# Last norm moved into the attention stage and into the expert blocks of a transformer layer with a mixture of experts

## What is computed

```python
mod = (_silu(c) @ wmod).reshape(16, 6, 1, -1)
sa, ca, ga, sb, cb, gb = (mod[:, 0], ..., mod[:, 5])
h = _layernorm(x) * (1 + ca) + sa
x = x + ga * attention(h, Wq, Wkv_down, Wk_up, Wv_up, Wo)
h = _layernorm(x) * (1 + cb) + sb
# router: top two of 8 experts, softmax over the two, 1280 rows an expert
y = einsum(gelu(einsum(h[tok], W1) + b1), W2) + b2
out = zeros_like(h).at[tok].add(y * gate) + h
x = x + gb * (layer_norm(out) * gamma + beta)
```

## Time and profile before

| | us |
|---|---|
| median of 3 runs | 1331.41 |
| lowest, highest | 1328.3, 1337.59 |
| span of the profiled execution | 1329.8 |
| its attention stage, to the last router sum | about 1031 |
| its routing | 1031 to 1115 |
| its expert blocks | 1115 to 1260 |
| last scatter and last norm | 1260 to 1329.8 |

### The profile page before, as it was taken

How to read it: one execution, slowest core, us unless ns; L and a number is a source line. 1 busy time by engine, 2 the same in 40 slices (tenths; PEclk the granted TensorE clock), 3 DMA queues, 4 the chain that set the end, 5 groups by cost and what they waited for, 6 DMA issues and landing times. The chain is left out here.

```text
span 1329.8 us, 23668 instructions
## 1 busy us (share of the span) xinstructions
PE 1153.5 (87%) x5959; PEld 770.8 (58%) x5960; DVE 975.3 (73%) x2248; ACT 748.2 (56%) x1454; POOL 936.3 (70%) x1075
## 2 busy tenths in 40 slices
PE   7899999999999999999999999999987127889800
PEld 5556566666666565666666665656554025889800
DVE  4888686777777776777777777867675897567676
ACT  4566656576566656665655666566642431344436
POOL 4586969687878869697878779697865203546438
PEclk9899999999999999999999999999998555899955
DMA  4000101010101101010101010010102412314196
GB/s 155 16 20 17 48 18 49 17 64 1 64 16 48 48 16 48 16 62 2 64 1 64 16 48 33 17 33 17 49 1 79 113 63 67 61 33 111 27 304 205
DMA packets 68478, 70.91 MB, mean 53 GB/s; under 512 B 12912, under 2 KB 64032, under 8 KB 68272
## 3 DMA queue, kind: packets, MB, share of 16 engines
q1 hardware_dynamic: 46800, 47.18, 11.0%
q10 hardware_dynamic: 16896, 16.78, 3.8%
q0 software_dynamic: 4704, 6.11, 2.9%
HBM read 40.35 MB, written 29.45 MB: 52 GB/s over the span
## 5 line engine op out<-in xcount | busy, mean ns | idle before, releaser
L717 ACT ACTIVATE PF<-PS 128x512 f32<-128x512 f32 x512 | 298.4, 595 | 256.7 <-PE PS L1124 248.5
L1016 DVE TENSOR_REDUCE NMAX<-PS 128x1 f32<-128x512 f32 x512 | 342.6, 682 | 88.5 <-PE PS L1133 84.8
L579 POOL TENSOR_TENSOR SF<-SF,PF 128x512 f32<-128x512 f32 x252 | 323.2, 1304 | 14.0 <-ACT PF L717 13.8
L1205 PE MATMUL PS<-PF,V 128*64 128x512 f32 x1024 | 248.0, 605 | 0.0
L1123 PE MATMUL PS<-Q,K 128*128 128x512 f32 x512 | 221.9, 433 | 2.6 <-ACT PF L717 2.5
L1133 PE MATMUL PS<-K,Q 128*128 128x512 f32 x512 | 205.8, 404 | 11.0 <-DVE NMAX L1016 10.9
L1124 PE MATMUL PS<-Q,K 128*128 128x512 f32 x512 | 201.5, 394 | 0.0
L736 ACT ACTIVATE Q<-PS 64x512 fp32r<-64x512 f32 x256 | 151.7, 593 | 48.2 <-PE PS L172 43.3
L656 POOL TENSOR_TENSOR XL<-XF,XH 128x512 fp32r<-128x512 f32 x63 | 82.9, 1316 | 131.1 <-ACT XH L794 131.1
L576 POOL TENSOR_TENSOR SF<-PF 128x512 f32<-128x512 f32 x126 | 162.4, 1305 | 5.8 <-ACT PF L717 5.3
L1123 PEld LDWEIGHTS PS<-Q,K 128*128 128x128 f32 x512 | 96.4, 188 | 120.0 <-issue 55.2
(11 more groups left out here) (361 smaller groups left out, 2427.2 us busy)
## 6 DMA issues: line engine op xcount, KB each, us to landing
X<-in_L_attn_x SPq DMA_DIRECT2D x16, 512.0 KB, 3.3
MODB<-mod_rows SPq DMA_DIRECT2D x16, 512.0 KB, 3.6
h_rows<-H ACTq DMA_DIRECT2D x16, 512.0 KB, 3.0
acc_rows<-H ACTq DMA_DIRECT2D x16, 512.0 KB, 4.1
out_x<-X SPq DMA_DIRECT2D x16, 512.0 KB, 2.9
A<-acc_rows SPq DMA_DIRECT2D x15, 512.0 KB, 8.9
W1F<-in_L_ffn_W SPq DMA_DIRECT2D x3, 1024.0 KB
W2F<-in_L_ffn_W SPq DMA_DIRECT2D x3, 1024.0 KB
```

What stands on the lines that cost most here:

```text
L579: s_sum.done(pool.tensor_tensor(total, total, tile, ALU.add))
L717: s_exp.done(act.activation(PF[:, u % 8, :], st_bank(u), ACT.Exp))
L1016: s_mred.done(dve.tensor_reduce(NMAX[:, p % 2, r:r + 1], mx_bank(u), AX.X, ALU.max, negate=True))
L1205: last = pe.matmul(num_bank(p)[odd * R:(odd + 1) * R, :], V1[:, vp, c, :], PF[:, k % 8, :], start=(c == 0), stop=(c == TC - 1))
```

## The change

The stage `last_norm` is gone, with its tiles. Its work goes to two places.

*Rows that no expert touches* get their last norm in the attention stage, and all rows are written that way. In batches 0 to 13: DVE takes statistics of `H2` (`base_stats`, four bn_stats and four bn_aggr), POOL makes the root for 12 columns in place of 8, ACT normalises `H2` into `BASEH`, DVE multiplies by `gb * gamma` (`blend`) and adds `X1` (`plus`), SP stores to `out_x`. Batches 14 and 15 are done in the routing, by POOL and ACT (`last_roots`, `last_bases`). `H2` has two buffers now; `NF` and `H2T` share a tile, and `BASEH` lies in `YT` and `LTF`. SP also writes `X1` and `gb * gamma` beside `H2` into `h2_rows`, whose rows grow from 1056 to 3104 bytes.

*Rows that an expert touches* are finished once more in the expert block. Block g gathers `XG` (3104 bytes a row), makes `YS` = accumulated row + expert's output, and stores it to `acc_rows` by a plain scatter; the next block gathers its own accumulated rows (`ACC`) from there, after that scatter has landed, before it can make its own `YS`. The norm of block g-1 (statistics, power on POOL, roots, normalise, scale, residual) runs within block g, and POOL scatters finished rows to `out_x`. A row with two experts is written twice. Rows of the next block are fetched, transposed and split in every block, also over the change of expert; half of the `HH` casts move from DVE to ACT, the `XTH` casts too.

The diff, cut to its core:

```diff
-h2_dram [NT + SPARES, D + E]
+h2_dram [NT + SPARES, ROW]        ROW = 3 * D + E, REST = D + E, BASED = NB - 2, XPS = 3
...
+    STAT3_AT, REST_AT, GIN_AT, XN3_AT = (62, 64, 66, 67), 76, 80, (85, 86, 87, 88)
+    BLEND_AT, PLUS_AT, BASE_AT = (88, 91), (92, 95), 96
 # sync, attention
+    for _, pb in due((REST_AT,), b, n):
...
+        s_gbb.wait(sp, pb, TC - 1)
+        s_rest.done(sp.dma_start(rows, X1[:, bass.ds(snap(sp, pb * TC), TC), :]))
+    for _, pb in due((BASE_AT,), b, n):
...
+                s_plus.wait(sp, pb, j)
+                s_base.done(sp.dma_start(token_rows(out)[...], BASEH[j]))
 # gpsimd, norm_scale
-    cols = slice(0 if new else TC, 2 * TC if old else TC)
+    cols = slice(0 if new else TC, 3 * TC if older else 2 * TC if old else TC)
 # scalar, attention
+    for c, pb in due(XN3_AT, b, n):
+        if based(pb):
+            s_norm.wait(act, scale_of(pb + 2), NORM_OPS - 1)
...
+            s_xn3.done(act.activation(BASEH[c // 2][:, c % 2, :], H2[:, ..., c, :], ACT.Identity,
+                                      scale=NY[:, col:col + 1], bias=NB1[:, col:col + 1]))
 # vector, attention
+    def base_stats(nb, c, jp):
...
+    def blend(pb, j):
+        s_blend.done(dve.tensor_tensor(BASEH[j], BASEH[j], BLEND[:, 0:1, :].broadcast_to([P, 2, D]), ALU.mult))
+    def plus(pb, j):
+        s_plus.done(dve.tensor_tensor(BASEH[j], BASEH[j], X1[:, bass.ds(pb * TC + 2 * j, 2), :], ALU.add))
 # route
+    def last_roots(pool):   # nine small operations on 8 columns, ahead of the constants
+    def last_bases(pool):   # four times a multiply and an add of 128x512, behind them
 # scalar, route, ahead of the first count
+        act.wait_ge(s_chain, CHAIN)
+        for c in range(LASTS * TC):
+            act.activation(X1[:, c, :], H2[:, c // TC, c % TC, :], ACT.Identity, ...)
 # gpsimd, experts
+        def block(e, g, k):
+            fetch(e, g + 1, k)       # waits s_t, s_gate, s_xp, s_stage of g; 2 gathers of XG
+            keep_sums(g)             # waits s_shift, s_y of g - 1; 2 scatters to acc_rows
+            power(g)                 # waits s_lch of g
+            store(g, 3)              # waits s_ladd of g - 1; 2 scatters to out_x
+            fetch_sums(g)            # waits s_sa of g; 2 gathers of ACC
 # scalar, experts, in block g
+                if f % 2:
+                    s_ho.done(act.activation(HH[:, f % 4, :], HF[:, f % 4, :], ACT.Copy))
+                if f == 4:
+                    normalise(g)
+                if f == 5:
+                    keep(g + 1)
+            turned(g + 1)
 # vector, experts, in block g
+                if f == 0:
+                    statistics(g)
+                if f == 1:
+                    moments(g)
+                    variances(g)
+                if f == 3:
+                    roots(g)
+                if f == 6:
+                    scale(g)
+            split_tokens(g + 1)
+            residual(g)
+            s_ga.wait(dve, g, 0)
+            for t in range(BT):
+                s_yb.done(dve.scalar_tensor_tensor(out=YB[:, t, :], in0=b2, scalar=GATES[:, t:t + 1], in1=ACC[:, t, :], ...))
+            if not more:
                 low_weights_1(dve, m, a + 1, 0)
-            s_sc.wait(dve, g + 2, BT - 1)
+            s_sa.wait(dve, g, 0)
             s_m2.wait(dve, g, FC - 1)
...
+            shift(g)                 # waits s_so of g; two small copies of the token lists
-def last_norm(nc, out, m, sem, sb, block):
...
```

More of the change, by code:

```diff
@@ L1758, in _, with keep, turned @@
+        each(pool, None, middle, last)
+        total = blocks(pool)
+        s_shift.wait(pool, total - 1, 1)
+        store(total, 3)
+        power(total)
+        store(total + 1, 2)
     @block.scalar
     def _(act):
+        def keep(g):
+            s_gx.wait(act, g, 0)
+            s_ladd.wait(act, g - 2, 0)
+            s_xp.done(act.activation(XP[:, kept(g), :], XG[:, :, REST:], ACT.Copy))
+        def turned(g):
+            s_t.wait(act, g, 0)
+            s_m1.wait(act, g, -1)
+            s_xh.done(act.activation(XTH[:, :, :], xt, ACT.Copy))
@@ L1760, in block, with normalise @@
+        def normalise(g):
+            s_lch.wait(act, g, 4)
+            s_lmul.wait(act, g, -1)
+            for t in range(BT):
+                s_lxn.done(act.activation(LX[:, t, :], YS[:, t, :], ACT.Identity, scale=LN[:, t:t + 1], bias=LNM[:, t:t + 1]))
         def block(e, a, g, k):
@@ L1777, in last @@
             high_weights_2(act, m, a + 1)
+        keep(0)
+        turned(0)
         each(act, None, block, last)
+        normalise(blocks(act))
     @block.vector
```

572 lines of the change are left out of this document (321 added, 251 removed).

## The result

The changed kernel takes 1379.83 us (median of four runs, 1378.97 to 1381.98); the kernel before took 1333.44 beside it. The ratio is 1.036, 95% interval 1.034 to 1.038: slower by 3.6%, outside the predicted range. The profiled execution has a span of 1380.3 us, 50.5 more than before.

| stretch | before, us | after, us | difference | predicted |
|---|---|---|---|---|
| first to last load of `MODB`, 15 batches | 903.67 | 961.75 | +58.1 | +14 |
| last load of `MODB` to the lists of tokens | 105.4 | 107.7 | +2.3 | +0.5 |
| lists to y(0) | 30.2 | 38.7 | +8.5 | +4 |
| y(0) to y(9) | 115.2 | 149.1 | +33.9 | +15 |
| y(9) to the end | 69.8 | 18.8 | -51.0 | -55.3 |

The account below looks back on a forecast made before the run. It took PE to bound attention and set the expert blocks' pace, the final norm being a stage by itself. 14 + 0.5 + 12.8 + 1 + 1.2 + 4 - 55.3 = -21.8 gave 1310 us on the runs' scale, range 1288 to 1337.

Parts of the forecast that it names:

- I cost DVE at nothing: Attention, batches 0 to 13: some 5 us of new DVE work per batch fits its 16 idle us, costing 0.
- Rival 2: Attention: DVE and POOL obstruct each other, 5.6 us more per batch on DVE, some 1.3 reaching PE; 1328 us; chance 0.16.
- ACT's 1.0 a batch: Attention: four added activations delay the exponentials PE waits for, 1.0 us a batch, 14 us in all (0 to 21).
- DMA ... nothing: Attention: 1.8 MB more per batch on queues 12% busy costs nothing.
- the chain: Expert blocks: y(g-1) through DRAM to y(g) adds 1.6 us to steps of 12.0, 12.8 over eight (0 to 27).
- the +1.2: Expert's last block: another `W1L` split stands between `YB` and `YS`, adding 1.2 us.
- Rival 3: Expert blocks: the way through DRAM becomes the bound, chain 18.4 us; slower by 21 us, 1353; chance 0.12.
- 20.4: Step between the experts: 13.6 + 5.6 for DVE's work before the statistics + 1.2, against 19.5 before.
- 34.2 forecast: Lists to y(0): larger first gather +1.5 and second gather meeting weights +2.5, 4 us together (2 to 8) over 30.2.
- End.: After y(9): 14.5 us with the waits instead of 69.8, closing with the last scatter's 3.84; -55.3 (-57 to -53).
- Routing.: Routing: added POOL and ACT operations fall in idle time, 0.5 us once for the first count; 4 if ACT uncovered.

Follow-up runs that it names:

- spread: Changed kernel with multiplications at slots 87 and 90, additions at 91 and 103, base store at 104, and an expert's first gates copied a block earlier: 1370.2 us.
- reslot: Changed kernel, same work, multiplications moved to slots 87 and 90, additions to 95 and 99, base store to 100: 1344.5 us; repeated unedited, 1354.8.
- no_blend_plus: Changed kernel with DVE's two multiplications and two additions per batch cut to one column each: 1329.7 us.
- no_xn3: Changed kernel without base rows in attention: no third normalisation, `blend`, `plus`, BLEND load or base stores, root on 8 columns: 1313.4 us.
- blend_95: spread with REST stores at slot 78, ACT's normalisations at 85, 87, 89, 91, multiplications at 90, 95, an unused power before ACC gathers: 1324.8 us, ratio 0.994.
- no_store: Changed kernel without the blocks' scatters of finished rows to `out_x`, the two at the end kept: 1362.1 us.
- no_store_2: spread with REST stores at slot 78 and without the blocks' scatters of finished rows to `out_x`: 1334.9 us.
- store_early: spread with REST stores at 78, normalisations at 87, 87, 89, 91, multiplications at 90, 99, finished rows scattered before the sums: 1335.5 us.

## Why the prediction was wrong

**"I cost DVE at nothing" failed**, and with it the largest term. The working took DVE's idle time in a batch (16 us) against 5 us of new work and the median 0.42 of the earlier trace rows, and set the 1.287 of the same rows, three times that, aside as a rival. In the units in question three of the four lines take 1.35 to 1.61 us in the median where 0.69 was taken, about twice. And it compared sums over a batch where a deadline counts: PE now waits up to 0.8 us at a time for the low halves of Q, and the clock falls behind these waits. Measured 2.7 us a batch where 0 was taken, 40 of the 58 us by which the stage grew. Rival 2 had the mechanism; its price of 1.3 was half, and what it left out is the clock: 1.8 of the 2.7 went when the clock came back. The Trainium skill, "SBUF — State Buffer", section "Who interferes with whom", says that such operations of DVE and GpSimd exclude each other; the trace agrees (1.38 and 1.61 against 0.69), and the wait can last over a whole run of GpSimd's operations, not one (7.74).

**ACT's 1.0 a batch was right**, in the mechanism too: 1.17 for ACT with root and base stores, over 15 intervals 17.6 us against 14. This is one difference between two runs, but the weight loads' waits for the exponentials show 1.4 a batch coming and going with ACT's four activations, as the prediction had said they would.

**"DMA ... nothing" held in this kernel only.** The queues had room, yet 1 MB ahead of a 4 KB transfer delayed it from 1.8 to 3.6 us, without a wait in after, and to over 7 in spread, at 1.4 us a batch.

**Steps: the chain was right where updates are punctual, but it is not what bounds after.** 13.6 forecast; 13.4 to 13.7 in reslot, no_blend_plus and no_xn3, with `YB` released by the landing as the chain has it (last block of an expert 14.3 to 14.6, the +1.2 less a little). After has 14.9 to 15.3: 1.4 a step from late updates of PE's semaphores, about 11 us in eight steps, which no row of before could show, and the rows of the chain are there 1.6 us or more before they are needed. Rival 3 (a DRAM chain of 18.4) is out: with punctual updates and no pause no step exceeds 13.8 but the last of an expert.

**The change of expert: "20.4" missed a wait.** The sum followed DVE and forgot what POOL's list begins with: the gather of the next rows, which waits for `NEXT` on DVE, behind turning loop and register reads. 26.9 measured. With that copy made early it is 19.8 to 20.9 in twelve variants, the forecast's 20.4. The same wait is in the start: 38.7 falls to 32.8 to 35.0, against 34.2 forecast. So one queue was left out, worth some 6 + 4.6 = 11 us. That the 20.4 then fits is in part luck: its sum ends with the gather of `ACC`, and in block 5 of all twelve that gather has landed 1.4 us or more before `YB` starts. In blend_95 it is the split of `W2L` (2.28 us) and PE's products behind it, at the lower clock (granted 0.60 from 1229 to 1237; 0.21 us each, later 0.12), that come last there.

**End.** -51.0 for -55.3: the sum let the span end with the landing of the last scatter, at 3.84. It lands after 2.4, but POOL's closing DRAIN takes until 5.7 us later, a term that the sum did not have. From the start of the last scatter to the end are 8.3 us in all variants but no_store and no_store_2 (6.7, with a DRAIN of 7.5), from y(9) 18.6 to 18.8 in all but store_early (17.7). What sets the length of the DRAIN is open.

**Routing.** +2.3 for +0.5, not tested.

In the sum: of the 72 us between forecast (-21.8) and measured (+50.5), attention holds 44, steps and change of expert 19, the start of the blocks 4.5, the end 4.3, the routing 1.8, and the start of attention gives 1.4 back. That attention is so much follows from the repetition: 14 batches multiply what one unit misses.

## What to carry to other kernels

Idle time of an engine over a batch says nothing of where it lies: for each operation that is added ask what stands behind it on its engine and how soon the bounding engine wants that, and price it by a row of its kind beside the same neighbour, not by the median over all places. A VectorE operation with two SBUF inputs belongs where GpSimd has gaps, and a small transfer that someone waits for ahead of large ones on its queue. When a stage is moved into others, its gain can be had (51 us here), but the repeated stages must be laid out anew: between the first and the last layout of the same work lie 55 us, 4 of them from the pause and 11 from the early gates.

## What the runs showed of the hardware

- A DVE operation of 128x512 with both inputs in SBUF: 0.69 us at best, 0.9 to 1.6 in the medians of the four lines beside a busy POOL, and 7.7 four times when POOL had no gap between its operations. Each of the four finished 0.55 us after POOL's run ended.
- The granted clock fell to 0.64 in a 4-us stretch (2.4 towards 1.2 GHz) after PE's short waits for the low halves of Q, each under 1 us, though PE was busy 3.68 of the 4 us before. Matmuls of 0.39 took 0.63. In spread PE was idle more, with waits up to 2.0 us, and the clock stayed at 1.00.
- Semaphore updates of PE up to 3 us late at the fifth and sixth indirect DMA issued in a row by POOL, in some executions and not in others of the same kernel. Its cause is open.
- Rows of 3104 bytes written in pieces: 512 KB took 9.6 and 10.6 us. A transfer of 4 KB on the same queue landed after 1.8 us when it went ahead of them, after 3.6 when issued 7.0 us behind the second, and after 7.1 to 8.1 when 4.3 us behind.
- A DRAIN of POOL of 8.4 and 9.1 us at the end of the program. In after it is the last thing that runs, 5.7 us beyond the last landing.
- A plain indirect scatter of 128 rows is issued in 1.0 us, one that accumulates in 1.62.
